# Shifted-window block: v from 98 compact token columns, odd tiles' rows moved by DMA, tokens tiled by pairs of windows, six transposes of norm 1

## The reference

```python
xn = layernorm(x, ln1_w, ln1_b)
xs = jnp.roll(xn, shift=(-SHIFT, -SHIFT), axis=(1, 2))
xw = xs.reshape(B, H // WS, WS, W // WS, WS, C)
xw = xw.transpose(0, 1, 3, 2, 4, 5).reshape(-1, N, C)
qkv = xw @ qkv_w + qkv_b
qkv = qkv.reshape(-1, N, 3, NH, hd).transpose(2, 0, 3, 1, 4)
q, k, v = (qkv[0], qkv[1], qkv[2])
attn = jnp.einsum('bhqd,bhkd->bhqk', q, k) * scale
attn = jax.nn.softmax(attn, axis=-1)
o = jnp.einsum('bhqk,bhkd->bhqd', attn, v)
# back to the image, then
x = shortcut + (o @ proj_w + proj_b)
h = jax.nn.gelu(layernorm(x, ln2_w, ln2_b) @ mlp_w1 + mlp_b1, approximate=False)
x = x + (h @ mlp_w2 + mlp_b2)
```

## Time and profile before

| | |
|---|---|
| median of three runs | 2984.17 us |
| profiled execution | 2986.28 us, its span 2984.1 us |
| mean granted clock of TensorE | 0.993 of full speed |
| busy share of the span: PE, PEld, DVE, ACT, POOL | 98%, 96%, 90%, 76%, 48% |
| DMA | 79.68 MB, mean 27 GB/s, 9.8% of 16 engines' span |
| loads and stores of x and out on SP | 640 + 640 issues, 147.0, 71.2, 54.8, 18.8 and 2.2 KB |

### The profile page before, as it was taken

One profiled execution on the slowest core, in us unless ns is written; L12 is line 12 of the kernel. 1 busy time (PEld: TensorE's weight loads), 2 busy tenths in 40 slices (PEclk: granted clock), 3 DMA queues, 4 the chain that ended last, 5 costly groups with the idle time before them and its releaser, 6 DMA issues.

```text
span 2984.1 us, 116983 instructions
## 1 busy us (share of the span) xinstructions
PE 2935.4 (98%) x43446; PEld 2865.3 (96%) x43446; DVE 2680.2 (90%) x6816; ACT 2266.7 (76%) x4472; POOL 1435.0 (48%) x1678
## 2 busy tenths in 40 slices
PE   5999999999999999999999999999999999999997
PEld 5999999999999999999999999999999999999997
DVE  5899999999999999999999999999999999999986
ACT  3778777777777777787777777777777877777774
POOL 2445444454544445454444545444454544445443
PEclk7999999999999999999999999999999999999999
DMA  1010010011001001100100110010011001000100
GB/s 47 25 29 24 24 31 26 24 27 29 24 24 30 26 24 27 29 24 24 31 26 24 27 29 24 24 30 26 24 27 29 24 24 30 26 24 27 30 21 18
DMA packets 109318, 79.68 MB, mean 27 GB/s; under 512 B 7294, under 2 KB 108782, under 8 KB 109294
## 3 DMA queue, kind: packets, MB, share of 16 engines
q1 hardware_dynamic: 108740, 78.56, 9.8%
q10 hardware_dynamic: 554, 0.79, 0.1%
HBM read 40.78 MB, written 38.54 MB: 27 GB/s over the span
## 4 chain that ended last, share of the span: by engine, by line
PE 97%; DVE 1%; issue 1%; DMA 1%; ACT 0%; POOL 0%; ACTq 0%; SPq 0%; DVEq 0%; POOLq 0%
PE ps L941 35%; PE ps L944 16%; PE ps L1053 5%; PE ps L972 5%; PE ps L1014 5%; PE ps L1026 5%; PE ps L1073 5%; PE ps L1027 5%; PE ps L1016 5%; PE ps L1015 5%; PE ps L903 3%; PE ps L911 2%; PE ps L1034 2%; PE ps L1038 1%; PE ps L913 1%
## 5 line engine op out<-in xcount | busy, mean ns | idle before, releaser
L426 POOL TENSOR_TENSOR gl<-g,gh 128x392 fp32r<-128x392 f32 x512 | 567.9, 1133 | 289.2 <-ACT gh L786 279.8
L941 PE MATMUL ps<-zh,w 128*128 128x392 f32 x3072 | 698.0, 342 | 0.6 <-ACT zh L738 0.6
L941 PEld LDWEIGHTS ps<-zh,w 128*128 128x128 f32 x3072 | 550.1, 188 | 0.8 <-ACT zh L738 0.8
L297 POOL TENSOR_TENSOR prob<-prob,rcp 128x588 f32<-128x588 f32 x128 | 152.2, 1189 | 746.2 <-DVE rcp L638 746.2
L780 ACT ACTIVATE g<-ps,biasf 128x392 f32<-128x392 f32 x768 | 397.4, 594 | 130.2 <-PE ps L941 130.2
L941 PE MATMUL ps<-zh1c,wqkv 128*128 128x392 f32 x1536 | 363.2, 345 | 11.0 <-DVE zh1c L488 11.0
L418 POOL CAST zh<-zh1c 128x392 fp32r<-128x392 f32 x256 | 134.0, 524 | 451.0 <-DVE z L478 434.6
L786 ACT ACTIVATE gh<-g 128x392 fp32r<-128x392 f32 x756 | 350.1, 552 | 0.0
L752 ACT ACTIVATE oh<-ps 128x392 fp32r<-128x392 f32 (+1 forms) x256 | 118.9, 521 | 279.1 <-PE ps L1073 279.1
L622 DVE TENSOR_TENSOR gl<-g,gh 128x392 fp32r<-128x392 f32 x256 | 289.8, 1170 | 5.7 <-ACT gh L786 5.7
L941 PEld LDWEIGHTS ps<-zh1c,wqkv 128*128 128x128 f32 x1536 | 281.1, 191 | 13.1 <-issue 11.6
(11 more groups left out here) (112 smaller groups left out, 7488.1 us busy)
## 6 DMA issues: line engine op xcount, KB each, us to landing
xin<-in_x SPq DMA_DIRECT2D x128, 147.0 KB
out<-yo SPq DMA_DIRECT2D x128, 147.0 KB
xin<-in_x SPq DMA_DIRECT2D x128, 71.2 KB
out<-yo SPq DMA_DIRECT2D x128, 71.2 KB
xin<-in_x SPq DMA_DIRECT2D x128, 54.8 KB
out<-yo SPq DMA_DIRECT2D x128, 54.8 KB
xin<-in_x SPq DMA_DIRECT2D x128, 18.8 KB
out<-yo SPq DMA_DIRECT2D x128, 18.8 KB
```

Of the source, the lines that this page charges most:

```text
L426: pool.tensor_tensor(gl[:, m, :], g[:, m, :], gh[:, m, :].bitcast(F32), ALU.subtract)\
L941: last = pe.matmul(dst, cols(w, part), act_, start=(n == 0), stop=(n == 4))
```

## The change

- Token tiles: a tile of 98 is now two neighbouring windows, seven image rows of 14 tokens. `moves` becomes one transfer for each of the seven rows over the tiles, and four for the ends at the cyclic shift: 11 transfers a load and 11 a store, `MOVES = WS + 4`.
- Norm 1 writes `z1` in the layout of `z2`, in six pieces instead of four, and is transposed in six matmuls instead of eight. The transposes multiply with `by_window`, the identity with its columns in window order, so that `zh1c` and `zl1c` are plain copies; the narrow ones are two half operations each.
- v takes its stationary columns from `zh1c` and `zl1c`, 98 for a pair. `values` copies all to `v_even`; SP moves the rows 49 to 97 to partitions 64 to 112 of `v_odd`, and `pv` reads even windows there and odd ones here, behind `v_moved`.
- `pad_windows`, `zh1`, `zl1` and their waits go.
- `qk` makes the two first passes of tiles 2 and 1 ahead of their other passes and waits for each part alone; GpSimd's `add_proj_bias` waits for `z2_done` where `pad_windows` did.

```diff
-MOVES = 5
+RUN = 2 * WS
+MOVES = WS + 4
@@ moves
-            turn = (WS - SHIFT) * SIDE - SHIFT
-            for lo, hi, src in ((0, turn, top + SHIFT), (turn, M - SHIFT, low), (M - SHIFT, M, top)):
-                while lo < hi:
-...
+            last = (BLOCKS - 1) * RUN
+            for row, rows, here, there in ((0, WS - SHIFT, top, low), (WS - SHIFT, SHIFT, low, top)):
+                for r in range(rows):
+                    p, at = RUN * (row + r), here + SHIFT + r * SIDE
+                    whole = BLOCKS - (r == rows - 1)
+                    yield p, RUN, slice(0, whole), at * C, [[C, RUN], [RUN * C, whole], [1, C]]
+                yield p, RUN - SHIFT, slice(BLOCKS - 1, BLOCKS), (at + last) * C, [[C, RUN - SHIFT], [1, C]]
+                yield p + RUN - SHIFT, SHIFT, slice(BLOCKS - 1, BLOCKS), there * C, [[C, SHIFT], [1, C]]
@@ sync, between load_x and store
+                wait(sp, v_ready, 1, i, 1)
+                sp.dma_start(v_odd[WIDE:PAIR, :, :], v_even[TOK:PART, :, :]).then_inc(v_moved, 16)
@@ gpsimd
-            def pad_windows(grp):
-...
-                    last = pool.tensor_copy(spaced(spread), packed(tight).bitcast(F32))
-                last.then_inc(zpad_done, 1)
...
-                if more(i):
-                    wait(pool, z2_done, 1, i - 1, 1)
-                    pad_windows(i + 1)
                 if more(i + 1):
                     rstd(mv1, ve1, rs1, mv1_done, ve1_done, rs1_done, i + 2, z1_done)
                 if more(i):
+                    wait(pool, z2_done, 1, i - 1, 1)
                     add_proj_bias(i + 1, 1 - parity)
@@ vector
+            def in_pairs(z):
+                pieces = []
+                for h in range(BLOCKS // 2):
+                    pieces += [(z[:, h, 0:C], 2 * h, slice(0, C)), (z[:, h, C:C + B], 2 * h + 1, slice(A, C)),
+                               (z[:, h, C + B:2 * C], 2 * h + 1, slice(0, A))]
+                return pieces
@@ low_parts1 (and likewise high_parts1)
-                dve.tensor_tensor(in_windows(zh1c[0:64, 1, :]), in_rows(ps[64:128, T1 + 1, 0:M]),
-                                  in_windows(zh1c[64:128, 1, :]).bitcast(F32), ALU.subtract).then_inc(zl1_done, 1)
+                for odd in range(2):
+                    hi, lo = slice(64 * odd, 64 * odd + 64), slice(64 - 64 * odd, 128 - 64 * odd)
+                    wait(dve, zh1_done, 3, grp, 2 + odd)
+                    last = dve.tensor_tensor(blocks_of(zh1c[lo, 1, :], odd), stacked(ps[hi, T1 + 1, 0:M // 2]),
+                                             blocks_of(zh1c[hi, 1, :], odd).bitcast(F32), ALU.subtract)
@@ transposes1
-                    for part in range(2):
-                        last = pe.transpose(ps[:, T1 + part, span(p)], z1[:, p, 64 * part:64 * part + 128],
-                                            ident[0:PART, 0:PART])
+                    a0 = (C + B) * (p % 2)
+                    pe.transpose(ps[:, T1, span(p)], z1[:, p // 2, a0:a0 + A], by_window[:, :])
+                for h in range(BLOCKS // 2):
+                    last = pe.transpose(ps[:, T1 + 1, span(h)], z1[:, h, A:A + 2 * B], by_window[:, :])
@@ qk
+                for t in tiles:
+                    tile(t, (0, 1), {0: [(zh1_done, 3, i, 1)]})
+                for t in tiles:
+                    tile(t, (2, 3, 4), {2: [(zl1_done, 2, i, 1)], 3: [(zh1_done, 3, i, 3), (zl1_done, 2, i, 2)]})\
@@ v
-                    last = project(ps[0:PAIR + 1, V + p // 2, 256 * (p % 2):256 * (p % 2) + C], zh1, zl1, wqkv,
+                    last = project(ps[0:PART, V + p // 2, 256 * (p % 2):256 * (p % 2) + C], zh1c, zl1c, wqkv,
                                    lambda w, part: w[:, part, 2 * C:3 * C],
-                                   tokens=slice(2 * WIDE * p, 2 * WIDE * p + PAIR + 1))
+                                   tokens=span(p))
@@ pv
-                wait(pe, v_ready, 1, i, 1)
+                wait(pe, v_moved, 16, i, 16)
-                                    last = pe.matmul(dst, vt[r, p, HD * h:HD * h + HD], pt[r, 2 * b + e, :], start=True,
+                                    last = pe.matmul(dst, (v_even, v_odd)[w][r, p, HD * h:HD * h + HD], pt[r, 2 * b + e, :], start=True,
@@ tensor, body
-                    qk(i + 1, (2,))
-                    qk(i + 1, (1, 0))
+                    qk(i + 1, (2, 1))
+                    qk(i + 1, (0,))
```

More of the change, by code:

```diff
@@ L23 @@
 PAIR = WIDE + TOK
-COLS = WIN * WIDE
 M = WIN * TOK
@@ L385, in _ @@
                                pattern=[[-1, 128]], channel_multiplier=1).then_inc(ident_ready, 1)
-            for t in (zh1[:, 0, :], zh1[:, 1, :], zl1[:, :]):
-                pool.memset(t.bitcast(F32).rearrange("p (w t) -> p w t", t=WIDE)[:, :, TOK:WIDE], 0.0)
+            pool.wait_ge(ident_ready, 2)
+            pool.tensor_copy(by_window[:, :].rearrange("p (w r c) -> p w r c", w=2, c=WS),
+                             ident[0:PART, 0:PART].rearrange("p (r w c) -> p w r c", w=2, c=WS)).then_inc(ident_ready, 1)
             pool.memset(qA[:, M:], 0.0)
@@ L482, in low_parts1 @@
             def low_parts1(grp):
[L484 to L487, removed]
-                dve.tensor_tensor(in_windows(zh1c[0:64, 1, :]), in_rows(ps[64:128, T1 + 1, 0:M]),
-                                  in_windows(zh1c[64:128, 1, :]).bitcast(F32), ALU.subtract).then_inc(zl1_done, 1)
+                wait(dve, zh1_done, 3, grp, 1)
+                dve.tensor_tensor(zl1c[:, :], ps[:, T1, 0:M], zh1c[:, 0, :].bitcast(F32), ALU.subtract).then_inc(zl1_done, 1)
+                for odd in range(2):
[3 more added lines that the diff above has]
+                                             blocks_of(zh1c[hi, 1, :], odd).bitcast(F32), ALU.subtract)
+                last.then_inc(zl1_done, 1)
             def low_wide2(grp):
@@ L519, in apply1 @@
                 wait(dve, t1_done, 1, grp - 1, 1)
-                pieces = [(z1[:, p, :], p, slice(0, C)) for p in range(BLOCKS)]
-                norm_apply(xin[:, parity, :, :], mv1, rs1, pieces, grp, mv1_done, rs1_done, z1_done)
+                norm_apply(xin[:, parity, :, :], mv1, rs1, in_pairs(z1), grp, mv1_done, rs1_done, z1_done)
             def columns(n, dst):
@@ L658, in apply2 @@
             def apply2(grp, parity):
[L660 to L663, removed]
                 wait(dve, t2_done, 1, grp - 1, 1)
-                norm_apply(x2[:, parity, :, :], mv2, rs2, z2_pieces, grp, mv2_done, rs2_done, z2_done)
+                norm_apply(x2[:, parity, :, :], mv2, rs2, in_pairs(z2), grp, mv2_done, rs2_done, z2_done)
             def body(i, parity):
@@ L729, in high_parts1 @@
                 wait(act, t1_done, 1, grp, 1)
-                act.activation(in_windows(zh1c[:, 0, :]), in_rows(ps[:, T1, 0:M]), ACT.Copy).then_inc(zh1_done, 1)
-                act.activation(in_windows(zh1c[64:128, 1, :]), in_rows(ps[64:128, T1 + 1, 0:M]), ACT.Copy)\
-                   .then_inc(zh1_done, 1)
+                act.activation(zh1c[:, 0, :], ps[:, T1, 0:M], ACT.Copy).then_inc(zh1_done, 1)
+                for odd in range(2):
+                    hi = slice(64 * odd, 64 * odd + 64)
+                    act.activation(blocks_of(zh1c[hi, 1, :], odd), stacked(ps[hi, T1 + 1, 0:M // 2]), ACT.Copy)\
+                       .then_inc(zh1_done, 1)
             def high_wide2(grp):
@@ L947, in qk, with tile @@
             def qk(i, tiles):
-                wait(pe, zh1_done, 2, i, 2)
-                wait(pe, zl1_done, 2, i, 2)
+                def tile(t, passes, waits={}):
+                    return project(ps[:, QK[t], 0:M], zh1c, zl1c, wqkv, lambda w, part: w[:, part, 128 * t:128 * t + 128],
+                                   passes=passes, waits=waits)
                 for t in tiles:
-                    project(ps[:, QK[t], 0:M], zh1c, zl1c, wqkv, lambda w, part: w[:, part, 128 * t:128 * t + 128])\
+                    tile(t, (0, 1), {0: [(zh1_done, 3, i, 1)]})
+                for t in tiles:
+                    tile(t, (2, 3, 4), {2: [(zl1_done, 2, i, 1)], 3: [(zh1_done, 3, i, 3), (zl1_done, 2, i, 2)]})\
                         .then_inc(qk_done, 1)
             def v(i):
-                wait(pe, zpad_done, 1, i, 1)
                 for p in range(PAIRS):
@@ L1110, in _ @@
             pe.wait_ge(w_lo, QKV + 1)
-            qk(0, (2,))
-            qk(0, (1, 0))
+            qk(0, (2, 1))
+            qk(0, (0,))
             pe.wait_ge(pads_ready, 2)
```

38 lines of the change are left out of this document (8 added, 30 removed).

## The result

The changed kernel takes 3008.1 us (median of four, 3006.74 to 3011.87), before 2984.45 in the same runs: ratio 1.0082, 95% interval 1.007 to 1.0094. Forecast were 3066 us and +2.7%. The measured time lies inside the stated range of 2945 to 3140 us and the direction held, but the size was three times too large, and the cause was another one.

A forecast was written before the change was run, and what follows sets the result against it. TensorE bounds the kernel before at 22.71 us a group; SP's issue ring would bound the changed one at 23.4. 2986.3 + 85 - 3 = 3068 us profiled, 3066 as a median; range 2945 to 3140.

The forecast's parts named there:

- TensorE's savings: On TensorE, v from compact columns saves 0.28 us a period and six transposes instead of eight 0.11: PE needs 22.32.
- VectorE alone then needs 21.5 + 0.55 = 22.05 us, still under PE's 22.32: VectorE's work a period without waits, plus 0.39 us for `apply1` and 0.16 for `low_parts1`, stays below TensorE's.
- cost of the longer `apply1` 0: On VectorE, `apply1` in six pieces adds 0.39 us ahead of the statistics, but VectorE still stays under PE's time.
- The ring over SP's issues: SP's stores, then x loads, norm statistics and next `yo` close in 23.4 us and set the period: +85 us, chance 0.65.
- Landing: From the last x load's issue on SP's queue to VectorE's norm 1 statistics: 1.5 us.
- VectorE's part behind the statistics: On VectorE, from the norm 1 statistics to the end of the next `yo`: 9.25 us.
- The rule against it: The skill's dispatch of about 50 ns per DMA: 12 more transfers cost 0.6 us, and SP's chain stays under PE's time.
- qk in two passes: TensorE's same 15 matmuls, the first four waiting only for the high wide part: no time gained as such.
- the transfer of v: SP moves v's odd tiles, 147 KB, landing 5 us or more before `pv` needs them: cost 0.
- pads, ScalarE: Three casts a group leave GpSimd, and ScalarE gets one small operation more with 22% to spare: both 0.
- rival 4: On SP's queue, transfers in flight block two to four issues of each set by 0.3 us: 3180 us, chance 0.12.
- rival 2: Small transfers issue faster, under 0.50 us apart, SP's chain stays hidden and PE bounds at 22.32: 2934 us, chance 0.17.

The follow-up runs named there:

- experiment 1: The kernel before with one edit, norm 1's `apply1` in six pieces instead of four: 3032.9 us, ratio 1.0155.
- experiment 9: The kernel before with the other PSUM banks and moved waits of experiment 7: 2982.1 us, ratio 0.9998.
- experiment 4: The changed kernel with each of the five loads of 14 partitions by four tiles split in two, 16 loads a group instead of 11: 3132.9 us, ratio 1.0497.
- experiment 7: The changed kernel with other PSUM banks, so TensorE's wait for `x` moves from `turn_probs` to norm 1's transposes and `qB`'s ahead of all scores: 2945.6 us, ratio 0.9879.
- experiment 6: The kernel of experiment 5 with GpSimd's first three gelu low parts held back until `apply1` is done: 3080.7 us, ratio 1.0332.
- experiment 5: The changed kernel with VectorE's two residual additions ahead of `apply1` instead of behind it: 3262.9 us, ratio 1.0929.

## Why the prediction was wrong

*TensorE's savings*: right in the sum, 0.21 + 0.17 us against 0.28 + 0.11. v's matmuls came to 93 ns each, not to the projection's 89.

*"VectorE alone then needs 21.5 + 0.55 = 22.05 us, still under PE's 22.32", cost of the longer `apply1` 0*: this step failed. The 0.38 us lie in a ring of VectorE and TensorE and cost 48 us where they are the only change (experiment 1). The step compared sums of work by engine and asked only which engine would be full. I listed the waits of SP for the pieces, but not that `turn_probs` waits for `x2`, behind `apply1` on VectorE. TensorE's full look hid it: matmuls overlap, so a wait of 0.1 us between their starts leaves the busy time at 700.00 of 700. In the groups between 1000 and 1200 us `turn_probs` took 1.26 us on average in the kernel before and 1.16 in that of experiment 9, where it doesn't wait for `x`.

The Trainium skill ("Perfetto Trace Analysis", "Identifying the Most-Contended Engine") says that the busy share of matmuls is not a good measure of how close a kernel is to the roofline, since they are pipelined. This case agrees in kind, by that 0.10 us in each group, which the matmuls' busy time did not show; the weight loads did not show it either (684.75 us of 700 before, 684.83 in experiment 9). A list of TensorE's waits from the code, each with the end of what it waits for beside it, has the end of `x` at 1519.55, in the middle of `turn_probs`.

*The ring over SP's issues, forecast at 0.65*: it exists, and with five more loads it decides (experiment 4), but its 23.4 us were too many by 2.0, so that it stays under the period. That the direction held is therefore luck: another ring lengthened it. Of the 2.0 the sets of eleven, 5.24 us and 5.35 instead of 5.6 each, make 0.6, since most issues are shorter than the 0.36 us of a set's first one, which I took for all of 14 partitions (median 0.32). Timeline of SP in the kernel after, first and last store, first and last load:

```profile
1519.00 0.37 SPq L341 DMA_DIRECT2D out<-yo  x1
...
1524.24 0.25 SPq L341 DMA_DIRECT2D out<-yo  x1
1525.03 0.35 SPq L320 DMA_DIRECT2D xin<-in_x  x1
...
1530.38 0.26 SPq L320 DMA_DIRECT2D xin<-in_x  x1
```

Landing makes 0.25, and VectorE's part behind the statistics the rest: I had taken over the gelu operations' length from a place where they ran beside GpSimd.

*The rule against it*: the section of the Trainium skill that I named ("DMA: Bandwidth & Descriptors", "Anatomy of one DMA") describes DMAs issued by GpSimd, and this kernel's are issued by SP. The issues of 0.25 to 0.37 us in the rows above speak against carrying its 50 ns over.

*qk in two passes, the transfer of v, pads, ScalarE*: no wait came of them. The waits view has no wait of `pv` for a DMA. *Issues that block* (rival 4): no load or store in the steady period shown is above 0.37, and the 0.85 of rows 4 is gone there. The faster side (rival 2, 2934 us) comes near once the other ring is shortened, 2945.6. Its condition, under 0.50 us from issue to issue, was not met (0.52 and 0.54 on average); SP's ring is short enough mainly because VectorE's part of it was 1.35 us shorter in experiment 4 than I had it.

*Open*: no run has `apply1` in four pieces together with six transposes, or `qB` out of the way, so how far below 22.41 us the period can go is not shown.

## What to carry to other kernels

When an engine is full and an edit takes work from it, close the rings before adding up: for every wait of that engine, write down when what it waits for ends, and which edits lie in that ring. An edit that saves where the ring does not pass is worth nothing (v: 0 or 27 us by the same code), and one that adds 0.38 us of cheap work on a second engine inside it is paid in full (48 us). Opening one ring can leave the next one just behind it, as the waits for `x` and `qB` in experiment 7 show. A second engine's duration may not be carried to another place in time without looking at what ran beside it.

## What the runs showed of the hardware

VectorE and GpSimd hold each other up by operation, not evenly. The six operations of `apply1` (SBUF to SBUF, one tensor operand) take 1.62 us alone and 3.75 beside GpSimd's `gl` operations. GpSimd's three keep theirs, 3.05 us. That `apply1` comes back to 1.62 us when only GpSimd's start is held back (experiment 6) shows the cause. The gelu low parts on VectorE (two SBUF operands) take 0.5 us each alone (1.01 for two) and have a mean of 1170 ns in the kernel before, where they ran beside GpSimd, and of 846 in the kernel after. There GpSimd pays too: its `gl` operation beside them took 1.44 us in the kernel before, where one takes 1.03 in the kernel after (GpSimd's timeline of the kernel before):

```profile
1523.10 1.44 POOL L426 TENSOR_TENSOR gl<-g,gh 128x392 fp32r<-128x392 f32 x1
```

The residual addition (one operand in PSUM) and the statistics did not change beside them: 1.02 us and 1.12 to 1.14 us in all rows. The Trainium skill ("SBUF — State Buffer", "SBUF: two separate sides") calls the port pair that VectorE and GpSimd share an exclusive lock for a whole instruction, taken by VectorE's operations in the two-port mode or with two SBUF inputs against a GpSimd operation that reads SBUF. The rows agree in which operations are held up; whether `apply1` runs in the two-port mode no row shows. Here it made the time self-correcting in one place: when VectorE came later, its gelu operations no longer met GpSimd's and the ring got shorter by up to 1.3 us.

TensorE's granted clock fell behind TensorE's waits in experiment 5, the kernel with the longest of them. TensorE stood 2.01 us in each of three groups in a row. Behind the third wait, which ended at 1562.16, the granted clock is 0.50 (the 1.2 GHz level) from 1564 to 1566 and 1.00 again from 1567, and `mlp2` takes 6.98 us instead of 5.41. The first two waits were as long, and the clock stayed at 1.00 behind them; why it is every third group is not shown. In the changed kernel, where `turn_probs` takes 1.82 us instead of 1.16 because of the wait, the clock stays at 1.00.
